# A two-layer decoder on one core: context products moved ahead of the routing of the first feed-forward

## The reference, cut to what matters

```python
x = x + _L0_attn_ref(_layernorm(x), ...)
x = x + _L0_xattn_ref(ctx_1024, _layernorm(x), mask_BxS2, ...)
x = x + _L0_ffn_ref(_layernorm(x), ...)
x = x + _L1_attn_ref(_layernorm(x), ...)
x = x + _L1_xattn_ref(_layernorm(x), ctx_1024, ctx_1024, ...)
x = x + _L1_ffn_ref(_layernorm(x), ...)

def _L0_ffn_ref(hidden_states, Wr, W1, b1, Wo, bo, gamma, beta):
    x = hidden_states.reshape(-1, H)
    expert_idx = argmax(softmax(x @ Wr.T))
    for e in range(E):                       # 8 experts, one for each row
        inter = inter + (expert_idx == e) * gelu(x @ W1[e] + b1[e])
    y = inter @ Wo + bo + x
    return layer_norm(y) * gamma + beta

def _L1_xattn_ref(q, k, v, mask, ...):       # k and v are the context
    Q, K, V = heads(q @ wq.T + bq), heads(k @ wk.T + bk), heads(v @ wv.T + bv)
    score = Q @ K.T / dk
    ctx = where(mask, -inf, score) @ V
    return layer_norm(q + ctx @ wo.T + bo)
```

## Time and profile before

| | us |
|---|---|
| median of three runs | 1867.79 (1864.09 to 1875.49) |
| the profiled execution, whole | 1861.0 |
| its span in the trace | 1859.2 |
| TensorE clock granted over the span | 0.965 |
| busy: PE / DVE / ACT / POOL | 1689.0 / 1009.9 / 740.9 / 658.7 |

### The profile page before, as it was taken

How to read it: one execution, slowest core, us unless ns; L and a number is a source line. 1 busy time by engine, 2 the same in 40 slices (tenths; PEclk the granted TensorE clock), 3 DMA queues, 4 the chain that set the end, 5 groups by cost and what they waited for, 6 DMA issues and landing times. The chain is left out here.

```text
span 1859.2 us, 32555 instructions
## 1 busy us (share of the span) xinstructions
PE 1689.0 (91%) x11198; PEld 1331.6 (72%) x11198; DVE 1009.9 (54%) x2462; ACT 740.9 (40%) x2093; POOL 658.7 (35%) x559
## 2 busy tenths in 40 slices
PE   7899899999999999999999967999889688886898
PEld 6677677777777777777777756899688466554666
DVE  5466465665555665665555532232363577655664
ACT  2255344454444444454444412343113566541210
POOL 1022245555444555554454514343500233352000
PEclk9899999999999999999999979999989799997999
DMA  3100200000000000000000035753300000010000
GB/s 95 54 1 1 98 22 10 10 10 9 9 9 0 9 9 9 9 9 9 9 3 6 1 102 170 246 182 123 103 20 1 1 1 1 1 56 1 0 20 20
DMA packets 48803, 67.39 MB, mean 36 GB/s; under 512 B 11826, under 2 KB 42770, under 8 KB 46034
## 3 DMA queue, kind: packets, MB, share of 16 engines
q1 hardware_dynamic: 47186, 62.66, 10.8%
q0 software_dynamic: 1536, 3.67, 0.6%
HBM read 57.02 MB, written 9.31 MB: 36 GB/s over the span
## 5 line engine op out<-in xcount | busy, mean ns | idle before, releaser
L688 POOL TENSOR_SCALAR l0x_p<-l0x_p,l0x_inv 112x488 f32<-112x488 f32 x256 | 387.2, 1524 | 365.6 <-DVE l0x_inv L782 365.6
L891 ACT ACTIVATE l0x_p<-l0x_s,l0x_low 112x488 f32<-112x488 f32 x256 | 178.4, 697 | 288.0 <-DVE l0x_low L771 288.0
L771 DVE CUSTOM_DVE_ANT_0 l0x_s<-l0x_score_ps,l0x_bias 112x488 f32<-112x488 f32 x256 | 160.3, 664 | 128.5 <-PE l0x_score_ps L1031 117.2
L758 DVE TENSOR_TENSOR l0x_kT_lo<-l0x_proj_ps,l0x_kT_hi 128x488 fp32r<-128x488 f32 x128 | 85.3, 667 | 104.3 <-ACT l0x_kT_hi L881 104.3
L1039 PE MATMUL l0x_pT_ps<-ident,l0x_p 112*122 112x112 f32 x1024 | 124.8, 262 | 13.9 <-POOL l0x_p L688 13.8
L1039 PEld LDWEIGHTS l0x_pT_ps<-ident,l0x_p 112*122 112x122 f32 x1024 | 107.8, 139 | 35.4 <-POOL l0x_p L688 22.8
L1904 POOL TENSOR_TENSOR l1a_pn<-l1a_p,l1a_inv 112x1792 f32<-112x1792 f32 x16 | 50.9, 3184 | 227.7 <-DVE l1a_inv L1932 227.7
L1052 PEld LDWEIGHTS l0x_oT_ps<-l0x_pT,l0x_v 122*64 122x64 f32 x2048 | 100.6, 138 | 43.1 <-issue 32.6
L1052 PE MATMUL l0x_oT_ps<-l0x_pT,l0x_v 122*64 122x112 f32 x2048 | 127.8, 267 | 3.9 <-DVE l0x_pT L777 3.1
L1979 ACT ACTIVATE l1a_p<-l1a_p,l1a_shift 112x112 f32<-112x112 f32 x256 | 95.3, 373 | 63.0 <-DVE l1a_shift L1926 63.0
L987 PE MATMUL l0x_proj_ps<-l0x_kvT_hi,l0x_wkv_hi 128*128 128x488 f32 x256 | 110.4, 431 | 3.0 <-DVE l0x_kvT_lo L746 3.0
(11 more groups left out here) (359 smaller groups left out, 3697.4 us busy)
## 6 DMA issues: line engine op xcount, KB each, us to landing
l0f_w<-in_l0f_w SPq DMA_DIRECT2D x21, 1024.0 KB
l0x_c_in<-in_ctx SPq DMA_DIRECT2D x16, 375.0 KB
l0f_context<-in_ctx SPq DMA_DIRECT2D x16, 375.0 KB
sorted_x<-l0x_zeros SPq DMA_DIRECT2D x1, 2816.0 KB, 14.9
l0f_xs<-sorted_x SPq DMA_DIRECT2D x21, 128.0 KB, 2.2
sorted_y<-l0f_ys SPq DMA_DIRECT2D x21, 128.0 KB, 1.7
l0x_wkv<-in_l0x_wkv SPq DMA_DIRECT2D x2, 1024.0 KB, 9.5
x<-in_x SPq DMA_DIRECT2D x4, 448.0 KB, 8.5
```

The lines of the kernel that those rows point to most:

```text
L688: nc.gpsimd.tensor_scalar(p[:, i % 2, a, :], p[:, i % 2, a, :], inv[:, i % 2, a:a + 1], None, ALU.mult).then_inc(pn_ready, 1)
L771: nc.vector.tensor_tensor_reduce(s_sb[:, h % 2, :], score_ps[0:S, h % 2, 0:KEYS], bias[:], -SCALE, 3.4e38, ALU.add, ALU.min, low[:, h:h + ...
L891: nc.scalar.activation(p[:, h // 2 % 2, h % 2, :], s_sb[:, h % 2, :], ACT.Exp, scale=-1.0, bias=low[:, h:h + 1], accum_out=total[:, h:h + ...
```

## The change

- A new class `GramOperands` holds the four context slots, `wk`, `wv`, the bias rows and `heads` for the rest of the program. SP loads them (nine DMAs) at the end of its own work in the **cross attention**; the ones beside the context are set by POOL at the start of that block.
- PE's order in the head becomes: half of Gram product 0, transposes, its other half, router product, Gram product 1, rank products, Gram products 2 to 5, six mixes.
- `EARLY` is 6: six batches in the head, ten in the tail.
- The load of the score mask (`l0f_masked`, read by DVE from tile 4 on) goes from SP's list in the head to the loop, i = 1.
- To make room, two raw copies of weights are released early, and layer 1's self attention keeps `x1`, `x2` and `x_new` in a buffer that is there already.

```diff
@@ class CrossAttentionWeights: open
-        self.affine, self.wkv = ph.sb("affine", [128, 4, KC]), ph.sb("wkv", [128, KC, 2 * INNER])
+        self.affine = ph.sb("affine", [128, 4, KC])
...
+        self.staging = ExitStack()
+        self.wkv = Phase(self.nc, self.staging, "l0x", side="right").sb("wkv", [128, KC, 2 * INNER])
+class GramOperands:
+    SLOTS = 4
+    def __init__(self, nc, ctx):
+        ph = Phase(nc, ctx, "l1x_gram")
+        self.context = ph.sb("context", [N // 3, self.SLOTS, 3, D + 1])
+        self.wk, self.wv = ph.sb("wk", [128, KC, D]), ph.sb("wv", [128, KC, D])
...
+    def context_load(self, A, n):
+        return self.context[:, n % self.SLOTS, :, 0:D], A["ctx"][n].rearrange("(c p) d -> p c d", p=N // 3)
+    def loads(self, A):
+        return ((self.wk[:], ...), (self.wv[:], ...), (self.kv_rows[:], ...), (self.k_bias[:], ...), (self.heads[:], ...),
+                *(self.context_load(A, n) for n in range(self.SLOTS)))
@@ l0_cross_attention, sync
             sp.wait_ge(padded, 16)
+            for part, source in gram_in.loads(A):
+                sp.dma_start(part, source).then_inc(gram_in_w, 16)
+            sp.wait_ge(gram_in_w, 16 * len(gram_in.loads(A)))
@@ l0_cross_attention, gpsimd
             nc.gpsimd.memset(zeros[:], 0.0).then_inc(zeroed, 1)
+            nc.gpsimd.memset(gram_in.context[:, :, :, D:D + 1], 1.0)
@@ l0_experts
-    EARLY = 5
+    EARLY = 6
@@ l0_experts, sync
             def load_context(n):
-                if n < 4:
-                    sp.wait_ge(ones_set, 1)
-                else:
-                    sp.wait_ge(gram_done, n - 3)
-                sp.dma_start(context[:, n % 4, :, 0:D], ...).then_inc(context_w[n % 4], 16)
+                sp.wait_ge(gram_done, n - 3)
+                part, source = gram_in.context_load(A, n)
+                sp.dma_start(part, source).then_inc(context_w[n % 4], 16)
...
-            sp.dma_start(wk[:], ...).then_inc(mix_w, 16)
-            (wv, kv_rows, k_bias, heads likewise)
-            for n in range(4):
-                load_context(n)
-            sp.dma_start(masked[:], A["score_mask"].rearrange("b s n -> s b n")).then_inc(mask_w, 16)
             clear_spent(sp, spent)
             for n in range(4, EARLY):
                 load_context(n)
@@ the loop over tiles, sync
+                if i == 1:
+                    sp.dma_start(masked[:], A["score_mask"].rearrange("b s n -> s b n")).then_inc(mask_w, 16)
@@ l0_experts, vector
-            dve.wait_ge(mix_w, 80)
@@ l0_experts, tensor
+            multiply_context(0, (0,))
             pe.wait_ge(x1_ready, B - BULK)
             (transposes of batches 14 and 15)
+            multiply_context(0, (1,))
             pe.wait_ge(xT_ready, 1)
             (router product)
+            multiply_context(1, (0, 1))
             pe.wait_ge(route_w, 48)
-            multiply_context(0)
             pe.wait_ge(route_step, 2 * B + 3)
             pe.wait_ge(rstd_step, 3)
             (rank products)
-            for n in range(1, EARLY):
-                multiply_context(n)
-            pe.wait_ge(mix_w, 80)
-            pe.wait_ge(xT_ready, 1)
+            for n in range(2, EARLY):
+                multiply_context(n, (0, 1))
             pe.wait_ge(route_step, ROUTED)
             make_mixes(0)
```

More of the change, by code:

```diff
@@ L1146, in l0_cross_attention, with l0_experts @@
     return ph.sems
-def l0_experts(nc, x, stats, norms, router, mix, flag, next_w, ident, passed, A, spent):
+def l0_experts(nc, x, stats, norms, router, gram_in, mix, flag, next_w, ident, passed, A, spent):
     E, F = 8, 1024
@@ L1188, in l0_experts @@
         y = x1
[L1189 to L1192, removed]
+        context, wk, wv = gram_in.context, gram_in.wk, gram_in.wv
+        kv_rows, k_bias, heads = gram_in.kv_rows, gram_in.k_bias, gram_in.heads
+        v_heads = ph.sb("v_heads", [128, KC, 128])
         gram, gram_k = ph.sb("gram", [128, GN, KC, D + 1]), ph.sb("gram_k", [128, 2, KC, D])
@@ L1304, in _ @@
         def _(pool):
-            nc.gpsimd.memset(context[:, :, :, D:D + 1], 1.0).then_inc(ones_set, 1)
             pool.wait_ge(mv_step, B - BULK)
@@ L1569, in _, with multiply_context @@
         def _(pe):
[L1570 to L1575, removed]
+            def multiply_context(n, parts):
+                if parts[0] == 0:
+                    since(pe, context_w[n % 4], 16 * (n // 4))
+                    if n == EARLY:
+                        pe.wait_ge(gelu_ready, 2 * TILES)
+                    since(pe, gram_ready, n - 1)
+                for c in parts:
                     for t in range(NC):
@@ L1578, in multiply_context @@
                                                 context[:, n % 4, t, :], start=(t == 0), stop=(t == NC - 1))
-                done.then_inc(gram_done, 1)
+                if parts[-1] == KC - 1:
+                    done.then_inc(gram_done, 1)
             def sum_keys(g):
@@ L1707, in __init__ @@
         self.wv = ph_in.sb("wv", [128, KC, DH])
-        self.wq, self.wk = ph_in.sb("wq", [128, KC, H * DH]), ph_in.sb("wk", [128, KC, 2 * DH])
+        self.wk = ph_in.sb("wk", [128, KC, 2 * DH])
         self.wq_hi, self.wq_lo = ph_in.sb("wq_hi", [128, KC, H * DH], F32R), ph_in.sb("wq_lo", [128, KC, H * DH], F32R)
+        self.staging = ExitStack()
+        self.wq = Phase(nc, self.staging, "l1q", side="right").sb("wq", [128, KC, H * DH])
     def loads(self, A):
@@ L2610, in program @@
             spent = l0_attention(nc, x, stats, norms, cross_w, ident, passed, A)
-            spent = l0_cross_attention(nc, x, stats, norms, cross_w, router, ident, passed, A, spent)
+            cross_w.staging.close()
+            gram_in = GramOperands(nc, ctx)
+            spent = l0_cross_attention(nc, x, stats, norms, cross_w, router, gram_in, ident, passed, A, spent)
         mix = ctx.enter_context(nc.sbuf_tensor("mix", [128, B, KC, 128], F32))
@@ L2617, in program @@
             attention_w = SelfAttentionWeights(nc, attention_ctx, projections)
-            l0_experts(nc, x, stats, norms, router, mix, flag, attention_w, ident, passed, A, spent)
-            l1_attention(nc, x, stats, norms, attention_w, projections, mix_w, ident, passed, A)
+            l0_experts(nc, x, stats, norms, router, gram_in, mix, flag, attention_w, ident, passed, A, spent)
+            attention_w.staging.close()
+            l1_attention(nc, x, stats, norms, attention_w, projections, mix_w, router[1], ident, passed, A)
         with ExitStack() as expert_ctx:
```

25 lines of the change are left out of this document (12 added, 13 removed).

## The result

The changed kernel takes 1851.4 us (median of 4 runs, 1851.1 to 1856.1), the kernel before 1871.6 in the same session (4 runs, 1864.1 to 1880.0): a ratio of 0.9895, 95% interval 0.985 to 0.994, so 20 us less, between 11 and 28. The forecast was 1848.8 in 1838 to 1861.

A forecast was written before the change was run, and what follows sets the result against it. PE, busy for 91% of the span, was taken as the bound, its branch ending the head last. Head -16.5, tail -6.1, loop +3.5 and memset +0.1 gave -19.0: 1848.8 us, range 1838 to 1861.

The forecast's parts named there:

- Up to the ranks: Head: matmuls from 1087, ranks done at 1095.4 (full clock) or 1100.2 (half) instead of 1107.5, gain 12.1 or 7.3 us.
- Rival 1: Head: TensorE runs at half clock as before; head gains 11.7, sum -14.2, time 1853.6 us; chance 0.14.
- Scatter branch: Head after the ranks: slot chain, scatter and first tile load unchanged, 30.4 us plus 0.3 to the transposes.
- rival 4: Head: DVE's mix steps stop POOL's scatter; the prediction argued this costs nothing; chance 0.05.
- PE's branch: Head after the ranks: four Gram products, then six mixes, 29.3 us to the transposes if undisturbed; the 5.3 wait goes.
- I keep this 4.7, since the scatter lies beside the mixes again: Head: mixes lose 4.7 us beside the scatter as before; transposes at 1129.4 or 1134.2, head gains 16.5.
- rival 3: Head: PE is held up all through the scatter, loss 13, head gains 8; sum -10.5, 1857.3 us; chance 0.09.
- Rival 2: Head and loop: unnamed waits may belong to weights' traffic and vanish, mask not late; sum -25.8, 1842.0 us; chance 0.18.
- Tail: Tail: one Gram product (3.5) and one mix (2.6) fewer on the path, gain 6.1 us, ends 5.2 and 6.6.
- Loop: Loop: context tiles may fill five DMA engines and make the mask late; loss 3.5 us, ends 0 and 5.
- Rival 5: Cross attention: new buffers' placement or traffic lengthens POOL's 256 steps; at 8% the kernel takes 1880 us; chance 0.04.
- The median scale: Whole kernel: profiled 1861.0 would become 1842.0; the runs' median 1867.8 lies 6.8 above, so 1848.8 us.

The follow-up runs named there:

- old_order: Changed kernel with PE's old order in the head, the early loads and six batches kept: 1853.7 us, ratio 0.9925.
- loads_in_head: Changed kernel with the nine early loads back in the head behind `wo`, new order and six batches kept: 1865.5 us, ratio 0.9962.
- no_scatter: Changed kernel without POOL's 16 scatter DMAs and SP's wait for them, so tiles read zeros: 1840.4 us.
- weights_after: Changed kernel with the first three experts' weights asked for after the scatter and the first tiles' loads: 1858.1 us.
- mask_in_head: Changed kernel with the mask's load moved from loop i = 1 back to the head, behind `wo`: 1850.8 us, ratio 0.9924.
- pause_once: Changed kernel with context loads split 112 and 13 partitions, and POOL waiting once after eight DMAs in scatter and gathers: 1839.3 us, ratio 0.9838.

## Why the prediction was right, and where it was not

The time came out 2.6 above the forecast, well inside the range. Against the mean of the two profiles of before the stages moved by -11.3 (head), +0.3 (loop) and -4.9 (tail), -15.8 together; the forecast had -16.5, +3.5, -6.1. Against its own terms the head gave 5.2 less and the tail 1.2 less, the loop cost 3.2 less. So that the time came out this close is in part luck: the head's loss beside the scatter was sized far too low, and the loop's error covered half of what came of it. The measured difference of medians, 20 with 11 to 28 around it, holds both sums.

- **Up to the ranks: right in each step.** Full clock, transposes behind the first half product, ranks 8.0 after PE's first matmul (forecast 8.4 after the start), 12.4 earlier than before (forecast 12.1), no wait for a context tile. Rival 1 (half clock) falls. old_order shows that the loads bring 8.8 of the 12.4 and the order the rest; loads_in_head shows that the order without them makes the ranks 3.6 later.
- **Scatter branch: right.** The tile's rows are in at 1131.02, 38.2 after PE's first matmul; forecast 30.4 + 8.4 + 0.3 = 39.1. The steps are 1.24 apart beside DVE's mixes, so rival 4 falls. Its price was also too high: of the five DVE steps of a mix only the two of L1474 read both inputs from SBUF. The rule of the Trainium skill, "SBUF — State Buffer", section on the two separate sides, speaks of such a step beside a GpSimd operation that reads SBUF; no hold of DVE on the scatter shows here.
- **PE's branch: the step that failed is "I keep this 4.7, since the scatter lies beside the mixes again".** The mechanism was kept, the size not: with the whole scatter beside the mixes the loss was 12.4 (30.2 against no_scatter's 17.8), and the transposes stood 49.3 after the first matmul instead of 42.4 after the start. That is rival 3, whose 13 was near and whose 9% was too little. The 4.7 was no constant to carry over: it was what remained of the standstill when PE began its mixes 12.3 us after the scatter's first DMA, against 4.9 now. The second profile of the kernel before lost 8.2 there. Rival 2's idea that the weights' traffic does it is refuted by weights_after.
- **Tail: right, a little less** (4.9 of 6.1). ACT's copies waited for "remote" in both kernels, 13.9 us in all before and 14.1 after, so the standstill beside the gathers stayed as it was, and only the product and the mix went.
- **Loop: the step that failed is the whole loss of 3.5 taken as new.** The five engines were rightly seen, and they cost 4.9 us (158.1 against 153.2). But before paid it too: its two profiles lie 5.5 and 3.6 above the same 153.2 (no run splits its loads). Its waits for tile rows came to 7.6 us, now 9.6, and begin one tile earlier. The mask's own price is 2.6 (mask_in_head), of which +0.3 shows in the stage; the two profiles of before lie 1.9 apart there, so the missing 2.3 is hardly more than their spread.
- **Rival 5 falls at its size.** Of the 5.5 us more of cross attention 1.6 go with the new allocation, by the batch's period (a term that the sum lacks); for the rest no row names a cause, and the two profiles of the kernel before lie 12.3 apart.
- **The median scale: luck.** The forecast time is the median of three runs, 1867.8, less 19.0. With a fourth run the median of before is 1871.6, so the forecast's base was 4 too low, and the measured difference, 20.2, is larger than the 19.0. By stages only 15.8 show. The profiled executions alone differ by 9.4, since the one of before lay 10 below its kernel's median; by their own scale (1842.0 forecast, 1851.6 measured) the forecast was 9.6 off.

## What to carry to other kernels

A stall that one profile shows beside a long transfer need not be its price once more of the work lies there (4.7 became 12.4 here): price it by the kernel without the transfer. Before moving a load, look at the DMA share of a lone one; if it sits at a fixed fraction, split the partitions so that more engines take part, which here was worth more than placing the mask. And where a row of indirect DMAs runs beside engines that hand work to one another, try a break in the row, and look at who waits for the row's end: here the later end cost PE a wait of 5.55 us and half clock in the first tile.

## What the runs showed of the hardware

- In a row of sixteen indirect DMAs at 1.24 us, hand-overs between PE, DVE and ACT came late, the first of them some 9 to 15 us after the first DMA and the last at most 4 us after the last had started, with idle waits of up to 14.2 us (ACT in the tail of weights_after); for 4 us of it no engine but POOL did anything. In the scatter rows of four and of eight held PE up by 0.4 us at most, but they are not free of it: a row of eight had one DVE step 4.4 late, and in the tail it left PE a wait of 3.02. POOL's own pace in the scatter is the same 0.94 + 0.30 throughout. Why it starts late in the row, and what in the chip holds the engines, no run here tells.
- PE's clock stayed full with half a Gram product in the hole at the block's start (weights_after, after the same stretch at half clock as old_order, to within 0.1 us). Without it it was at half from the transposes on in old_order, and right behind them in both profiles of the kernel before. In pause_once it fell within PE's wait of 5.55 us behind the mixes (1.00 until 1130, 0.50 from 1132) and was back at 1.00 only from 1142.
